# Where a token tile's LayerNorm units, its first projections and the first scores stand in a Trainium2 transformer layer

## The chip, the cores and the metric

The kernel runs on all 8 cores of one Trainium2 chip. Each core computes one of the 8 sequences (2048 tokens of width 1024) with its own copy of the weights; the cores exchange nothing. The metric is device microseconds of the slowest core. Engines have short names: PE is the matrix engine, PEld its weight loads, DVE the vector engine, ACT the scalar engine, POOL and SP two engines that here mostly issue DMAs.

## The reference, cut to what matters

```
x = x + attention(layernorm(x))       # 8 heads of 128, softmax inside blocks of 64 tokens
x = x + spikes(layernorm(x))          # 1024 -> 4096 -> 1024 with squared relu
# attention: q = xn Wq + bq, k = xn Wk + bk, v = xn Wv + bv
#            softmax(q k^T / sqrt(128)) v  per block of 64 tokens, then Wo, bo
# spikes:    h = relu(xn W_fc^T)^2, y = h W_proj^T, five steps of a threshold unit on y
```

Inputs and weights arrive in float32. Weights are turned to bf16 by the DMAs that load them.

## The kernel before

**Tiles and stages.** The 2048 tokens of a core are four tiles (p = 0 to 3) of 512, and a tile is four row units of 128 tokens; unit i belongs to tile i // 4. A unit is loaded as 128 rows of x, normalized and transposed into a quarter of the tile `xnt[p % 2]`. In attention each tile needs 8 q groups, 8 k groups (one per head), 8 v groups and 8 o groups. A group is 8 matmuls of 512 columns into one of three PSUM banks, `ps_m`, which go round. Then come the two matrices of the feed-forward part, whose matmuls are the larger part of the time.

**Order of the work.** Nothing is planned at run time. Each engine has one program in order, and all of them walk the same list: block b = -1 is the q and k groups of tile 0 (`block_keys(-1)`: q0, k0, q1, k1, ... q7, k7 at s = 0 to 15); block 0 is q and k of tile 1 for heads 0 to 3 (s = 0 to 7), v of tile 0 (s = 8 to 15), q and k of tile 1 for heads 4 to 7, and v of tile 1, and then tile 0's o groups. In block b the scores, softmax and values of tile b are woven in between the groups at fixed places: `scores(b, 0)` (heads 0 to 3) stands before s = 0 and `scores(b, 1)` before s = 8 (`scores_four`, L82). The text below writes q0 to k7 for the groups of tile 0 and q(1,0), k(1,0), q(1,1), k(1,1) for the first of tile 1.

**How a unit goes through the engines.** Four steps: `ln_stats` on DVE (L654: two BATCH_NORM_STATS2 and an aggregate), `ln_rstd` on ACT (L554: Ln, then Exp), `ln_scale` on DVE (L662: subtract and multiply into `xn`), and `turn_x` on PE (L344: 8 transposes), whose result `turn_copy` on ACT (L561) copies into `xnt`. Units 4 to 7, those of tile 1, have their places in block -1: `EARLY_TURNS = (8, 11, 13, 15)` says before which s PE transposes them, and `ln_unit` (L133) sets the stats three places earlier, the rstd two, the scale one. Their transposes and that of unit 0 go to the single bank `ps_t`: the next transpose waits until the copy of the one before is done (`turn_free`, L340). Units 1 to 3 have banks of their own.

**Halves.** The first three groups of tile 0 (`HALVED = 3`) are made in halves of 256 tokens (L373): the first halves of q0, k0 and q1, with the transposes of units 2 and 3 between them, and then the second halves. Later tiles' groups take all 512 tokens at once and wait at the tile's first group for all four units (L363).

**ACT's other work.** ACT empties every q and k group with a bias (L566), in the order of the list, and makes the exponentials of the softmax. In its program the copy of a transposed unit stands before the emptying of its place's group, and the rstd of a unit just before the emptying of its group as well.

**Loads.** POOL issues the weights: Wq and Wk head by head, two heads deep (the load of head h waits until that of head h - 2 has landed, L857 to L864), then the two halves of Wv, each behind one of the last two k weights (L866). SP issues the first four units of x, then units 4 to 7 into `xs`, each behind one k weight: unit 4 + i behind head i + 1 (L951). Behind them on SP stand `bo` (waits for the second half of Wv), and the loads `xl` of units 8 onward.

Of the kernel before, what the change touches and what calls it, by code (L numbers as in the profile page):

```python
# [102 lines left out]

HALVED = 3


# [18 lines left out]

EARLY_TURNS = (8, 11, 13, 15)  # L130


def ln_unit(b, s, step):  # L133
# [22 lines left out]
def turn_order():  # L156

    keys = [("x", 0)]
    for b in range(-1, 4):
        for s in range(len(block_keys(b))):  # L160
            if (i := ln_turn(b, s)) is not None:
                keys.append(("x", i))
            if (j := turn_p_pair(b, s)) is not None:
                keys.append(("pt", b, j))
    return {k: n for n, k in enumerate(keys)}


def build_nc():
# [83 lines left out]
    ld_xs = [sem(f"ld_xs{i}") for i in range(4)]  # L252
# [62 lines left out]
    def turned_copied(i):  # L315
        return (free_x, i) if 1 <= i <= 3 else (free_t, turn_no[("x", i)] + 1)
# [22 lines left out]
    def tensor_program(E):  # L339
# [32 lines left out]

        def q_or_k_half(key, half):  # L373

            kind, _, h = key
            w_sb, loaded = (wq_sb, ld_wq) if kind == "q" else (wk_sb, ld_wk)
            if half == 0:
                E.wait_ge(loaded[h], 16)
            if key == ("q", 0, 0):
                E.wait_ge(*turned_copied(2 * half))  # L380
                E.wait_ge(*turned_copied(2 * half + 1))
            for c in range(8):
                k0 = h * 1024 + c * 128
                m = E.matmul(bank(key)[:, half * 256:(half + 1) * 256], w_sb[:, k0:k0 + 128],
                             tokens(xnt[0], c, 2 * half, 2), start=(c == 0), stop=(c == 7))
            return m

        def v_group(key):
# [116 lines left out]
        turn_x(1)  # L505
        for _ in range(WARM_AGAIN):
            E.matmul(ps_m[2][:], attn_sb[:, 0:128], attn_sb[:, 0:512], start=True, stop=True)
        for s, key in enumerate(block_keys(-1)[:HALVED]):
            q_or_k_half(key, 0)
            if s < 2:  # L510
                turn_x(2 + s)
        for b in range(-1, 4):
            for s, key in enumerate(block_keys(b)):
                if (i := ln_turn(b, s)) is not None:
                    turn_x(i)
                if (j := turn_p_pair(b, s)) is not None:
                    turn_p(b, j)
                if (f := scores_four(b, s)) is not None:
                    scores(b, f)
                if (f := values_four(b, s)) is not None:  # L520
                    values(b, f)
                if b == -1 and s < HALVED:
                    q_or_k_half(key, 1).then_inc(filled(key)[0], 1)
                else:
                    main(key)
            if b >= 0:
                for tt in range(4):
                    for half in range(2):
                        main(("o", b, tt, half))
# [23 lines left out]
    def scalar_program(E):  # L553
        def ln_rstd(i):  # L554
            E.wait_ge(ve_var, i + 1)
            E.activation(lnv[i % 2][:], mv[i % 2][:, 1:2], ACT.Ln,  # L556
                         bias=eps_sb[:, 0:1]).then_inc(ac_ln, 1)
            E.wait_ge(ac_ln, i + 1)
            E.activation(rstd[i % 2][:], lnv[i % 2][:], ACT.Exp, scale=-0.5).then_inc(ac_rstd, 1)

        def turn_copy(i):  # L561
            E.wait_ge(*turned(i))
            E.copy(ln_tile(i // 4)[:, i % 4 * 1024:(i % 4 + 1) * 1024],
                   turn_bank(i)).then_inc(turned_copied(i)[0], 1)

        def main(key):  # L566
            E.wait_ge(*filled(key))
            if key[0] == "q":
                h = key[2]
                if key == ("q", 0, 0):  # L570
                    E.wait_ge(ve_bqs, 1)
                    E.wait_ge(ld_bias, 16)
                m = E.activation(q_sb[:, h * 512:(h + 1) * 512], bank(key)[:], ACT.Identity,  # L573
                                 bias=bqs_sb[:, h:h + 1], scale=DKS)
            elif key[0] == "k":
                h = key[2]
                m = E.activation(k_sb[:, h * 512:(h + 1) * 512], bank(key)[:], ACT.Identity,  # L577
                                 bias=bias_sb[:, 8 + h:9 + h])
            else:
                m = E.activation(h_sb[key[2]][:], bank(key)[:], ACT.Relu)  # L580
            m.then_inc(emptied(key)[0], 1)

        def exps(p, j):
            E.wait_ge(free_s, 4 * p + j + 1)
            E.activation(e_sb[:], e_sb[:], ACT.Exp).then_inc(ac_exp, 1)

        def store_x2(p, tt):
            for half in range(2):
                E.wait_ge(*emptied(("o", p, tt, half)))
            j = 4 * p + tt  # L590
            E.dma_start(out=x2_h[j * 128:(j + 1) * 128, :], in_=xr[tt][:]).then_inc(st_x2[tt], 16)

        def value_copy(p, h):
            E.wait_ge(full_v, 4 * p + h // 2 + 1)
            src = bass.AP(values_bank(h)[:].tensor, (h % 2) * 256,
                          [[1024, 128], [512, 2], [64, 4], [1, 64]])
            dst = bass.AP(attn_sb[:].tensor, h * 512, [[4096, 128], [64, 2], [128, 4], [1, 64]])
            E.activation(dst, src, ACT.Identity,
                         bias=bias_sb[:, 16 + h:17 + h]).then_inc(free_v, 1)

        E.dma_start(out=bias_sb[:], in_=bias_h).then_inc(ld_bias, 16)

        E.wait_ge(ve_eps, 1)
        E.activation(table_sb[:], eps_sb[:], ACT.Ln)
        ln_rstd(0)
        ln_rstd(1)
        turn_copy(0)
        turn_copy(1)
        ln_rstd(2)
        ln_rstd(3)  # L610
        turn_copy(2)
        turn_copy(3)
        for b in range(-1, 4):
            for s, key in enumerate(block_keys(b)):
                if (i := ln_turn(b, s)) is not None:
                    turn_copy(i)
                if (f := values_four(b, s)) is not None:
                    value_copy(b, 4 * f)
                    value_copy(b, 4 * f + 1)
                if (i := ln_unit(b, s, LN_RSTD)) is not None:  # L620
                    ln_rstd(i)
                if key[0] != "v":
                    main(key)
                if f is not None:
                    value_copy(b, 4 * f + 2)
                    value_copy(b, 4 * f + 3)
                if (j := softmax_pair(b, s)) is not None:
                    exps(b, j)
            if b >= 0:
                for tt in range(4):  # L630
                    store_x2(b, tt)
        for fc in range(EARLY_UP, 32):
            main(("up", 0, fc))
        for t in range(4):
            if t > 0:
                for fc in range(32):
                    main(("up", t, fc))
            if t < 3:
                i = 20 + 4 * t
                for j in range(4):  # L640
                    ln_rstd(i + j)


    def vector_program(E):
# [119 lines left out]
        for b in range(-1, 4):  # L764
            keys = block_keys(b)
            added = {}
            for s, key in enumerate(keys):
                if (j := softmax_pair(b, s)) is not None:
                    softmax_shift(b, j)
                if (j := turn_p_pair(b, s)) is not None:  # L770
                    p_copy(b, j)
                if (i := ln_unit(b, s, LN_SCALE)) is not None:
                    ln_scale(i)
                if b >= 0 and (i := ln_unit(b, s, LN_BLOCKS)) is not None:
                    ln_blocks(i)
                if (i := ln_unit(b, s, LN_STATS)) is not None:
                    ln_stats(i)
                if s > 0 and (j := softmax_pair(b, s - 1)) is not None:
                    softmax_scale(b, j)
                if key[0] == "v":  # L780
                    v_copy(key)
                if b == 3 and s > 0:
                    square(0, s - 1)
                if b >= 0 and s >= len(keys) - 4:
                    tt = s - (len(keys) - 4)
                    added[tt] = add_bo(b, tt)
# [40 lines left out]
    def gpsimd_program(E):  # L827
# [35 lines left out]
                E.wait_ge(ld_wk[h - 2], 16)  # L863
            w_load(wk_sb[:, hs], wk_h[h], ld_wk[h])  # L864
        for half in range(2):
            E.wait_ge(ld_wk[6 + half], 16)  # L866
            w_load(wv_sb[:, half * 4096:(half + 1) * 4096], wv_h[half], ld_wv[half])

        E.wait_ge(*filled(("v", 0, 0, 0)))
# [36 lines left out]
    def sync_program(E):  # L906
# [41 lines left out]
        for tt in range(4):  # L948
            xr_load(0, tt)
        for i in range(4):  # L950
            E.wait_ge(ld_wk[i + 1], 16)  # L951
            E.dma_start(out=xs[i][:], in_=rows(x_h, 4 + i)).then_inc(ld_xs[i], 16)
        E.wait_ge(ld_wv[1], 16)
        E.dma_start(out=bo_sb[:], in_=bass.AP(bo_h.tensor, 0, [[0, 128], [1, 1024]])).then_inc(ld_bo, 16)
# [113 lines left out]
```

## Time and profile before

| | us |
|---|---|
| time, median of 3 runs (range) | 709.55 (709.0 to 710.76) |
| the profiled execution's own time | 708.54 |
| its span, slowest core (core 2) | 706.9 |
| spans of the 8 cores | 704.4 to 706.9 |
| PE busy in core 2 | 690.8 (98% of the span) |
| DVE, ACT, POOL busy | 384.3, 171.1, 49.9 |
| mean granted clock of PE, all cores | 0.997 to 0.999 of full speed |

The span runs from a core's first to its last instruction. It is shorter by 1.64 us than the time of that execution. An engine's busy share of the whole span says little about a stage, so the rows below are read in order of time: each row of a timeline is a run of equal instructions with its start, the length from the start of the first to the end of the last, and in brackets how long the engine sat idle before it and what released it.

### The profile page before, as it was taken

Reading aid. Unit: us, or ns where it says so; the run is one execution under the profiler, and the core shown is the slowest. Engines: PE = TensorE matmul, PEld = TensorE weight load, DVE = VectorE, ACT = ScalarE, POOL = GpSimd, SP = SyncE. Lnnn points to the kernel's source line nnn. Section 1 sums busy time; section 2 is a strip of 40 time slices with the busy share of each in tenths; the row PEclk is TensorE's granted clock in tenths of the full one; section 3 lists DMA queues with packets and bytes.
Section 4 is the critical chain, followed back from the end, with each engine's and each line's share of the span. In section 5 each row is a group of like instructions: output and inputs, shape, how many; then the busy total and the mean of one; then the engine's idle time right before and its main releaser. Section 6 shows DMA issues by size and latency. Waiting matters only on the chain.

```text
span 706.9 us, 10613 instructions; the slowest of 8 cores (704.4 to 706.9 us)
## 1 busy us (share of the span) xinstructions
PE 690.8 (98%) x3765; PEld 325.0 (46%) x3804; DVE 384.3 (54%) x573; ACT 171.1 (24%) x314; POOL 49.9 (7%) x96
## 2 busy tenths in 40 slices
PE   7999999999999999999999999999999999999996
PEld 3544444444444444444444444444444444444444
DVE  5235765786687466337755226845225865221476
ACT  3553330450351145030003331002332001332000
POOL 2211110121005100000000000000000000000000
PEclk9999999999999999999999999999999999999999
DMA  8997986598659994496361002262002042100011
GB/s 182 195 166 147 168 154 182 120 215 205 157 183 191 254 214 88 136 179 181 108 190 59 1 1 60 62 206 89 1 1 61 36 143 79 40 1 1 31 45 45
DMA packets 31010, 80.92 MB, mean 114 GB/s; under 512 B 5616, under 2 KB 5872, under 8 KB 30192
## 3 DMA queue, kind: packets, MB, share of 16 engines
q0 software_dynamic: 12960, 31.46, 25.4%
q1 hardware_dynamic: 15552, 40.39, 19.3%
q10 hardware_dynamic: 2448, 8.40, 3.0%
q8 instruction: 32, 0.52, 0.3%
q14 instruction: 18, 0.15, 0.1%
HBM read 82.33 MB, written 16.78 MB: 140 GB/s over the span
## 4 chain that ended last, share of the span: by engine, by line
PE 92%; DMA 5%; DVE 1%; issue 1%; DVEq 0%; POOLq 0%
PE ps_m L422 31%; PE ps_y L494 30%; PE ps_m L369 13%; PE ps_m L409 8%; PE ps_m L395 8%; DMA wq_sb<-Wq 5%; DVE acc_sb L738 1%; PE ps_y L448 1%; PE ps_y L476 1%; PE ps_t L460 1%; PE ps_m L501 0%; DVE acc_sb L735 0%; PE ps_t L351 0%; DVE xr L743 0%; DVE attn_sb L753 0%
## 5 line engine op out<-in xcount | busy, mean ns | idle before, releaser
L422 PE MATMUL ps_m<-xn2t,w_sb 128*128 128x512 bf16 x1024 | 223.0, 379 | 0.1
L494 PE MATMUL ps_y<-w_sb,h_sb 128*128 128x512 bf16 (+1 forms) x1001 | 216.4, 376 | 1.2
L422 PEld LDWEIGHTS ps_m<-xn2t,w_sb 128*128 128x128 bf16 x1024 | 99.7, 98 | 119.3 <-issue 0.2
L494 PEld LDWEIGHTS ps_y<-w_sb,h_sb 128*128 128x128 bf16 x1024 | 100.2, 98 | 117.6
L580 ACT ACTIVATE h_sb<-ps_m 128x512 bf16<-128x512 f32 x128 | 76.4, 597 | 267.9 <-PE ps_m L422 267.9
L728 DVE TENSOR_TENSOR h_sb<-h_sb 128x512 bf16<-128x512 bf16 x128 | 53.1, 424 | 125.8 <-ACT h_sb L580 125.7
L738 DVE SCALAR_TENSOR_TENSOR acc_sb<-ps_y,acc_sb 128x1024 bf16<-128x1024 f32 (+2 forms) x72 | 78.6, 1092 | 7.9 <-DVE acc_sb L735 0.5
L369 PE MATMUL ps_m<-xnt,wq_sb 128*128 128x512 bf16 x240 | 56.7, 379 | 2.3 <-DMA wq_sb<-Wq 2.3
L369 PE MATMUL ps_m<-xnt,wk_sb 128*128 128x512 bf16 x248 | 58.6, 379 | 0.0
L395 PE MATMUL ps_m<-wv_sb,xnt 128*128 128x512 bf16 x248 | 55.5, 379 | 0.8 <-issue 0.6
L409 PE MATMUL ps_m<-wo_sb,attn_sb 128*128 128x512 bf16 x249 | 55.4, 379 | 0.4
L735 DVE TENSOR_SCALAR acc_sb<-ps_y 128x1024 bf16<-128x1024 f32 (+2 forms) x18 | 19.5, 1084 | 63.7 <-PE ps_y L494 63.6
L573 ACT ACTIVATE q_sb<-ps_m,bqs_sb 128x512 bf16<-128x512 f32 x32 | 22.0, 686 | 78.1 <-PE ps_m L369 76.3
L409 PEld LDWEIGHTS ps_m<-wo_sb,attn_sb 128*128 128x128 bf16 x256 | 25.0, 98 | 30.2
L723 DVE TENSOR_TENSOR xr<-ps_m,xr 128x512 f32<-128x512 f32 x32 | 22.1, 690 | 29.5 <-PE ps_m L409 29.5
L395 PEld LDWEIGHTS ps_m<-wv_sb,xnt 128*128 128x128 bf16 x256 | 24.6, 98 | 28.5
L369 PEld LDWEIGHTS ps_m<-xnt,wq_sb 128*128 128x128 bf16 x240 | 22.7, 98 | 29.4 <-issue 3.4
L369 PEld LDWEIGHTS ps_m<-xnt,wk_sb 128*128 128x128 bf16 x248 | 23.7, 98 | 26.6 <-issue 0.2
L678 DVE STREAM_TRANSPOSE blk<-xn 128x1024 bf16<-128x1024 bf16 x24 | 29.8, 1241 | 1.5
L709 DVE CAST v_sb<-ps_m 128x512 bf16<-128x512 f32 x32 | 21.8, 685 | 14.1 <-PE ps_m L395 14.1
L556 ACT ACTIVATE lnv<-mv,eps_sb 128x1 f32<-128x1 f32 x32 | 9.4, 293 | 82.3 <-DVE mv L660 82.3
L577 ACT ACTIVATE k_sb<-ps_m,bias_sb 128x512 bf16<-128x512 f32 x32 | 22.0, 687 | 23.5 <-PE ps_m L369 23.2
(63 smaller groups left out, 340.2 us busy)
## 6 DMA issues: line engine op xcount, KB each, us to landing
xr<-x SPq DMA_DIRECT2D x32, 512.0 KB, 6.9
xl<-x SPq DMA_DIRECT2D x96, 128.0 KB, 4.1
w_sb<-Wfc POOLq DMA_DIRECT2D x32, 256.0 KB, 8.9
x<-xr ACTq DMA_DIRECT2D x16, 512.0 KB, 5.2
out<-xr POOLq DMA_DIRECT2D x12, 512.0 KB, 2.9
w_sb<-Wpr POOLq DMA_DIRECT2D x16, 256.0 KB, 32.7
xn2t<-blk SPq DMA_DIRECT2D x64, 64.0 KB, 2.0
w_sb<-Wpr POOLq DMA_DIRECT2D x4, 1024.0 KB, 15.1
```

The costliest lines, as they stand in the source:

```text
L369: m = E.matmul(bank(key)[:], w_sb[:, k0:k0 + 128], tokens(xnt[p % 2], c, 0, 4), start=(c == 0), stop=(c == 7))
L395: m = E.matmul(bank(key)[:], xnt[p % 2][:, tt * 1024 + c * 128:tt * 1024 + (c + 1) * 128], wv_sb[:, k0:k0 + 512], start=(c == 0), stop=(c ...
L409: m = E.matmul(bank(key)[:], attn_sb[:, h * 512 + tt * 128:h * 512 + (tt + 1) * 128], wo_sb[:, k0:k0 + 512], start=(h == 0), stop=(h == 7))
L422: m = E.matmul(bank(key)[:], w1_sb[fc // 4][:, k0:k0 + 128], tokens(xn2t, c, 0, 4), start=(c == 0), stop=(c == 7))
L494: return E.matmul(out, h_sb[fc][:, tt * 128:(tt + 1) * 128], w2_sb[fc // 4][:, k0:k0 + n], start=(fc == 0), stop=(fc == 31))
L573: m = E.activation(q_sb[:, h * 512:(h + 1) * 512], bank(key)[:], ACT.Identity, bias=bqs_sb[:, h:h + 1], scale=DKS)
L577: m = E.activation(k_sb[:, h * 512:(h + 1) * 512], bank(key)[:], ACT.Identity, bias=bias_sb[:, 8 + h:9 + h])
L580: m = E.activation(h_sb[key[2]][:], bank(key)[:], ACT.Relu)
L678: E.transpose(dst[:, :, :, u, :], xn[i % 2][:].rearrange("p (c a t) -> p c a t", c=8, a=4)).then_inc(ve_blk, 1)
L723: E.tensor_tensor(xr[tt][:, hs], bank(key)[:], xr[tt][:, hs], ALU.add).then_inc(emptied(key)[0], 1)
L728: E.tensor_tensor(h_sb[fc][:], h_sb[fc][:], h_sb[fc][:], ALU.mult).then_inc(ve_sq, 1)
L738: m = E.scalar_tensor_tensor(acc, y, level, acc, ALU.is_gt, ALU.add)
```

## The change

Five edits, all of them in the first 60 us of the program.

1. The transposes of units 4 and 5 move from before s = 8 and 11 of block -1 to before s = 11 and 14 (k5 and q7); their stats, rstd and scale move with them.
2. Units 6 and 7 leave block -1. On DVE `ln_stats`, `ln_scale` of unit 6 and then of unit 7 stand at the start of block 0. On ACT `ln_rstd(6)`, `ln_rstd(7)`, `turn_copy(6)`, `turn_copy(7)` stand at the end of block -1, behind the emptying of k7. On PE their transposes stand behind the first halves below.
3. The first three groups of tile 1, q(1,0), k(1,0) and q(1,1), are made in halves of 256 tokens like those of tile 0: the first halves need units 4 and 5 only, and the transposes of units 6 and 7 follow the first and the second of them; then come the second halves.
4. `scores(0, 0)` moves from the start of block 0 to before q6 (s = 12) of block -1. The softmax of these scores stays where it was, in block 0.
5. Units 4 to 7 are asked for behind the k weights of heads 2, 3, 5 and 6 instead of 1, 2, 3 and 4. The halves of Wv wait for units 6 and 7 (`ld_xs[2]`, `ld_xs[3]`) instead of the k weights of heads 6 and 7.

```diff
+FIRST_SCORES = (-1, 12)
-EARLY_TURNS = (8, 11, 13, 15)
+EARLY_TURNS = (11, 14)
@@ turn_order
+        if b == -1:
+            keys += [("x", 6), ("x", 7)]
@@ q_or_k_half
             if half == 0:
-                E.wait_ge(loaded[h], 16)
-            if key == ("q", 0, 0):
-                E.wait_ge(*turned_copied(2 * half))
-                E.wait_ge(*turned_copied(2 * half + 1))
+                if p == 0:
+                    E.wait_ge(loaded[h], 16)
+                main_free(key)
+            if kind == "q" and h == 0:
+                E.wait_ge(*turned_copied(4 * p + 2 * half))
+                E.wait_ge(*turned_copied(4 * p + 2 * half + 1))
@@ tensor_program
-        for s, key in enumerate(block_keys(-1)[:HALVED]):
-            q_or_k_half(key, 0)
-            if s < 2:
-                turn_x(2 + s)
         for b in range(-1, 4):
             for s, key in enumerate(block_keys(b)):
+                if (b, s) == FIRST_SCORES:
+                    scores(0, 0)
+                if b < 1 and s == 0:
+                    for n, halved in enumerate(block_keys(b)[:HALVED]):
+                        q_or_k_half(halved, 0)
+                        if n < 2:
+                            turn_x(4 * (b + 1) + 2 + n)
...
-                if (f := scores_four(b, s)) is not None:
+                if (f := scores_four(b, s)) is not None and (b, s) != (0, 0):
                     scores(b, f)
...
-                if b == -1 and s < HALVED:
+                if b < 1 and s < HALVED:
                     q_or_k_half(key, 1).then_inc(filled(key)[0], 1)
@@ scalar_program, behind the groups of a block
+            if b == -1:
+                ln_rstd(6)
+                ln_rstd(7)
+                turn_copy(6)
+                turn_copy(7)
@@ vector_program, ahead of the groups of a block
+            if b == 0:
+                for i in (6, 7):
+                    ln_stats(i)
+                    ln_scale(i)
@@ gpsimd_program
-            E.wait_ge(ld_wk[6 + half], 16)
+            E.wait_ge(ld_xs[2 + half], 16)
             w_load(wv_sb[:, half * 4096:(half + 1) * 4096], wv_h[half], ld_wv[half])
@@ sync_program
-            E.wait_ge(ld_wk[i + 1], 16)
+            E.wait_ge(ld_wk[(2, 3, 5, 6)[i]], 16)
             E.dma_start(out=xs[i][:], in_=rows(x_h, 4 + i)).then_inc(ld_xs[i], 16)
```

## Rows read from the trace of the kernel before

**Rows 1.** The cores: span and mean granted clock, two of eight.

```profile
core 2: 706.9 us, clock 0.998
core 6: 706.4 us, clock 0.999
```

**Rows 2.** Stretches of core 2: length, busy time by engine, PE clock, DMA share, GB/s.

```profile
10.00:12.00 2.00, 0.49 (x8) 0.46 (x8) 1.82 (x4) 0.50 (x2) 0.00 (x0) 1.00 1.06 176
30.00:40.00 10.00, 8.68 (x52) 4.20 (x51) 3.80 (x7) 5.04 (x10) 2.11 (x4) 1.00 1.06 217
140.00:706.00 566.00, 558.79 (x2914) 259.97 (x2944) 306.92 (x445) 120.45 (x222) 28.13 (x52) 1.00 0.40 102
```

**Rows 3.** Timeline of PE, core 2, units 1 to 3 and the first groups.

```profile
12.28 0.61 PE L351 MATMUL ps_y<-ident,xn 128*128 128x128 bf16 x8 [0.17 <-DVE xn L669]
...
17.69 0.61 PE L351 MATMUL ps_y<-ident,xn 128*128 128x128 bf16 x8
...
19.55 1.03 PE L384 MATMUL ps_m<-xnt,wq_sb 128*128 128x256 bf16 x8 [0.38 <-ACT xnt L563]
...
22.16 1.89 PE L369 MATMUL ps_m<-xnt,wk_sb 128*128 128x512 bf16 x8
23.89 1.89 PE L369 MATMUL ps_m<-xnt,wq_sb 128*128 128x512 bf16 x8
```

**Rows 4.** The same timeline: q5, q6, then unit 7, k7, the scores, q(1,0).

```profile
36.34 1.89 PE L369 MATMUL ps_m<-xnt,wq_sb 128*128 128x512 bf16 x8 [0.76 <-DMA wq_sb<-Wq]
...
41.47 1.89 PE L369 MATMUL ps_m<-xnt,wq_sb 128*128 128x512 bf16 x8 [0.99 <-DMA wq_sb<-Wq]
...
47.09 0.61 PE L351 MATMUL ps_t<-ident,xn 128*128 128x128 bf16 x8
47.53 1.89 PE L369 MATMUL ps_m<-xnt,wk_sb 128*128 128x512 bf16 x8
49.35 0.79 PE L448 MATMUL ps_y<-k_sb,q_sb 128*64 128x64 bf16 x32
50.08 1.90 PE L369 MATMUL ps_m<-xnt,wq_sb 128*128 128x512 bf16 x8
```

**Rows 5.** Timeline of PE, core 6: k1 and q(1,0).

```profile
22.39 1.89 PE L369 MATMUL ps_m<-xnt,wk_sb 128*128 128x512 bf16 x8
...
49.53 1.90 PE L369 MATMUL ps_m<-xnt,wq_sb 128*128 128x512 bf16 x8
```

**Rows 6.** DMA queues of core 2 up to 100 us: packets, MB, share of 16 engines.

```profile
q0 software_dynamic: 4333, 9.47, 61.9%
q1 hardware_dynamic: 2256, 7.34, 26.2%
```

**Rows 7.** Landing times of the tile xs (first row) and of wv_sb (second).

```profile
DMA to landing us min/median/max: 7.4/8.2/9.2
DMA to landing us min/median/max: 10.7/12.1/13.5
```

**Rows 8.** Timeline of POOL, core 2: the issue of the first half of Wv.

```profile
43.22 0.53 POOL L829 DMA_DIRECT2D wv_sb<-Wv  x1 [3.82 <-DMA wk_sb<-Wk]
```

**Rows 9.** Timeline of ACT, core 2: the emptying of q4 and of k7.

```profile
33.95 0.69 ACT L573 ACTIVATE q_sb<-ps_m,bqs_sb 128x512 bf16<-128x512 f32 x1 [1.30 <-PE ps_m L369]
...
49.52 0.69 ACT L577 ACTIVATE k_sb<-ps_m,bias_sb 128x512 bf16<-128x512 f32 x1 [0.58 <-PE ps_m L369]
```

**Rows 10.** Timeline of DVE, core 2: scales and stats of units.

```profile
10.45 1.68 DVE L669 TENSOR_SCALAR xn<-xr,mv,rstd 128x1024 bf16<-128x1024 f32 x2
...
26.60 0.69 DVE L657 BATCH_NORM_STATS2 stat<-xs 128x6 f32<-128x512 f32 x1 [9.40 <-DMA xs<-x]
...
29.06 0.81 DVE L669 TENSOR_SCALAR xn<-xs,mv,rstd 128x1024 bf16<-128x1024 f32 x1 [0.86 <-ACT rstd L559]
...
35.28 0.81 DVE L669 TENSOR_SCALAR xn<-xs,mv,rstd 128x1024 bf16<-128x1024 f32 x1 [1.74 <-ACT rstd L559]
...
75.14 0.68 DVE L657 BATCH_NORM_STATS2 stat<-xl 128x6 f32<-128x512 f32 x1
```

More of the change, by code:

```diff
@@ L373, in q_or_k_half @@
         def q_or_k_half(key, half):
-            kind, _, h = key
+            kind, p, h = key
             w_sb, loaded = (wq_sb, ld_wq) if kind == "q" else (wk_sb, ld_wk)
             if half == 0:
-                E.wait_ge(loaded[h], 16)
-            if key == ("q", 0, 0):
-                E.wait_ge(*turned_copied(2 * half))
-                E.wait_ge(*turned_copied(2 * half + 1))
+                if p == 0:
[4 more added lines that the diff above has]
+                E.wait_ge(*turned_copied(4 * p + 2 * half + 1))
             for c in range(8):
@@ L384, in q_or_k_half @@
                 m = E.matmul(bank(key)[:, half * 256:(half + 1) * 256], w_sb[:, k0:k0 + 128],
-                             tokens(xnt[0], c, 2 * half, 2), start=(c == 0), stop=(c == 7))
+                             tokens(xnt[p % 2], c, 2 * half, 2), start=(c == 0), stop=(c == 7))
             return m
```

## The prediction

> **What bounds the kernel now.** The spans of the cores come first [rows 1], then stretches of core 2 [rows 2]. From 140 us to the end PE is busy 558.8 of 566 us at full clock, so nothing there can be gained or lost except by a shift of the whole. Between 30 and 40 us it is busy only 8.68 of 10 us while the DMA share is full. The PE timeline says why: k1 begins at 22.16 and a group is 1.73 behind the one before it (23.89 - 22.16) [rows 3]. From k1 to k7 there are 12 groups (20.7 us) and four transposes of 0.44 (47.53 - 47.09), so k7 could begin at 44.6. It begins at 47.53: 2.9 us are lost, and q5 and q6 show to what, weights that had not landed [rows 4]. Behind k7 PE runs without a hole to the last matmuls. A test of this: from the start of k(1,1), three groups behind q(1,0), to the end it is 706.9 - 50.08 - 5.18 = 651.6 in core 2 and 706.4 - 49.53 - 5.18 = 651.7 in core 6 [rows 1, 4, 5]. So the forecast needs one number per core, when k(1,1) begins; 651.65 is added to it.
>
> **Part 1, the halves.** The matmuls are the same in number of columns. The last three halves of tile 0 take 22.16 - 19.55 = 2.61, 0.87 each, half of 1.73 [rows 3]. Six halves cost 5.2 like three groups: nothing, on the path or off it. The halves are there to let PE begin tile 1 with two units of four.
>
> **Part 2, the scores and transposes that move.** The 32 small matmuls take 0.73 (50.08 - 49.35) [rows 4] wherever they stand. They need only heads 0 to 3, emptied long before s = 12. DVE looks at them no earlier than now, since its first softmax step stays in block 0, now behind units 6 and 7. Nobody waits for it: PE's next need of it is before s = 8, eight groups on. Zero, with that cover; both ends are 0 to 0.2. Units 4 and 5 are transposed three places later than now, and their rstd lies behind the emptying of q4 and k5, three groups or more before PE wants them: zero.
>
> **Part 3, the loads.** The unit loads leave the stretch in which PE starves. Up to 100 us POOL's queue moved 9.47 MB in 61.9 us of all engines' time and SP's 7.34 MB in 26.2 [rows 6]. A head of Wq or Wk (0.26 MB written) is then 1.7 us and a unit of x (0.52 MB) 1.87 us. Before q5's weights, which land just ahead of 36.34, DMA now carries units 4, 5 and most of 6; after, only 4 and 5. That is 0.85 x 1.87 = 1.6 us earlier, 34.7. PE wants q5 at 22.16 + 7 x 1.73 = 34.3, so 0.5 us of wait remains. Further on two units fewer lie ahead of q6 and one or so ahead of k7, and PE has by then the scores and the transpose of unit 4 before q6: no more wait. The remaining loss r is 0.5, between 0 and the 2.9 of today. So k7 begins at 22.16 + 20.7 + 0.88 (two transposes) + 0.73 (scores) + r = 44.5 + r, where it is 47.5 now. SP's queue has bo and the loads of units 8 and 9 behind this, POOL's the halves of Wv and Wo. The second half of Wv goes out when unit 7 has landed, some 3 us later than now, and takes 10.7 to 13.5 us [rows 7], so it is there by 62; PE wants it after 70. Unit 8 then lands before 71 and DVE wants it at 75.14 [rows 10]. Zero, with 4 us or more of cover; without that each us late would cost one.
>
> **Part 4, what is late next.** Units 6 and 7 now stand behind k7 on every engine, and here new waits arise. I count from the start of k7.
> - ACT may begin `ln_rstd(6)` only behind the emptying of k7, which starts 49.52 - 47.53 = 1.99 behind k7 [rows 4, 9]. From the emptying to the next unit's scale on DVE it is 35.28 - 33.95 = 1.33 [rows 9, 10], the scale takes 0.81, and PE starts a transpose 0.15 after (12.28 against 10.45 + 1.68) [rows 3, 10]. So unit 6 can be transposed at 4.28. PE is at that place at 1.73 + 0.87 = 2.60. **Wait A: 1.7 us.**
> - DVE does unit 6's scale before unit 7's stats. The stats start at 4.13, the scale follows 29.06 - 26.60 = 2.46 later [rows 10], ends at 7.40, and PE may start at 7.55. ACT's copy of unit 6 stands behind `ln_rstd(7)` in its order, and the single bank makes PE wait for that copy too; it ends at about the same time. PE is there at 4.28 + 0.44 + 0.87 = 5.59. **Wait B: 2.0 us.**
> - From the transpose of unit 3 to the second half of q0 it is 19.55 - 17.69 = 1.86 [rows 3]. The second half of q(1,0) thus starts at 9.41, and PE is done with the first half of q(1,1) at 8.86. **Wait C: 0.55 us**, the same as the idle 0.38 printed in the row of q0.
> - k(1,1) begins at 9.41 + 2.61 = 12.02. Behind PE in wait A stand only its own groups; ACT has q(1,0) to empty afterwards and the exponentials, two groups ahead of the bank's next use.
>
> **The sum.** The start of k(1,1) is k1 + 20.7 + 0.88 + 0.73 + r + 12.02 = k1 + 34.35 + r. Core 2: 22.16 + 34.35 + 0.5 = 57.0, against 55.3 now: 3.05 us of weights and of shorter way are won less r, 4.2 us of waits come in. Span 57.0 + 651.65 = 708.7, which is 1.8 above 706.9. Core 6 has k1 at 22.39 [rows 5] and has to wait less for q5: 708.4 to 708.9. The slowest core is about 708.7. The profiled execution would take 708.54 + 1.8 = 710.3. The median shown is 1.0 above that execution, so with the same shift it is 709.55 + 1.8 = **711.3 us**. Against r from 0 to 1.0 and waits that are each some tenths off, the forecast's own range is 710.3 to 712.4.
>
> **Where a page of the skill bears on it.** Units of x landed 7.4 to 9.2 us after they were asked for [rows 7], though each is 1.87 us of work: SP's queue got about a third of the engines' time beside POOL's. The Trainium skill, DMA: Bandwidth & Descriptors, section on queues, rings and completion order, says that each engine takes packets in turn from the rows that have work. By equal turns a unit would land sooner than the row shows, and unit 7 would come some 2 us earlier; the time would be the same, and only the second rival would lose its chance. The row decides.
>
> **Rivals.**
> 1. Units 6 and 7 are ready in time, and only the gain remains. Then k(1,1) stands at k1 + 30.2 + r: 4.2 us less, 707.2. For it speaks that the loads of both are asked for some 9 and 4 us before k7; against it that not the loads but the order on ACT and DVE sets waits A and B, and no row of a step is shorter. Parts of it (a wait half as long) end between 707.2 and 710.
> 2. Slower: unit 7's load is late. It goes out when k6's weights land: now 42.7 (POOL's next issue, 43.22, less its own half us [rows 8]), after the change 1.2 unit loads less lie ahead, so 40.5. With 7.4 to 9.2 us to land [rows 7] it is there at 47.9 to 49.7. DVE is ready for it at k7 + 4.13 = 49.1. Only beyond that does each us late add one to wait B; at 9.2 us plus a late k6 it is 0.6 to 2 us, so 712 to 713.3, in the middle 712.4. What speaks against: unit 7 has at most k7's and q7's weights beside it, fewer than the loads of today had.
> 3. The weights come no earlier, because the engines' time, not the order, is short and the two first unit loads still fall among heads 3 to 5: r is 2.5, 713.3.
> 4. The clock. In the stretch of 10 to 12 us PE is busy 0.49 of 2 us and the granted clock is 1.00 [rows 2]; waits A and B leave no emptier stretch. If the clock fell to its lower level (1.2 of 2.4 GHz), the groups behind k(1,0) would take twice 1.73; for two or three groups that is 3.5 to 5 us, 715 to 716. The Trainium skill, TensorE: Matmul & The Clock Gate, section on why this matters for your kernels, says that a long idle gap between bursts brings the clock down; the row above shows a gap of 1.5 us which didn't.
>
> **Chances.** Forecast 0.64, rival 1 or a part of it 0.13, rival 2 0.15, rival 3 0.05, rival 4 0.03. A measurement of this kernel can tell about 0.3%, 2.1 us, from no change: faster is below 707.4, slower above 711.7. Faster: half of rival 1, 0.06. Slower: some 0.19 of the forecast's own upper part, 0.13 of rival 2, rivals 3 and 4: 0.40. Within: 0.54. The forecast lies within, with its upper end just beyond the bound. The range leaves out rival 4, the end of rival 3 and the lower part of rival 1: 709.3 to 713.1.
>
> **What would show it.** In the profile after: k7 at about 45 in core 2 with one or no wait for weights before it (part 3); PE waiting for DVE's xn at two transposes in `ps_t` behind it, near 1.5 and 1.8 us as printed, and for ACT's xnt once, near 0.4 (part 4); the Ln of unit 6 right behind the emptying of k7; 12 us from k7 to k(1,1); and still 651.65 from there to the end. The stats of unit 7 released by a DMA instead of by DVE's own order would be rival 2; a scale of unit 6 before k7 ends would be rival 1. The forecast is wrong if a core other than 2, 5 or 6 starts k1 much later than 22.4, since every us of k1 is one of the time.

## The result and the profile after

The changed kernel takes 711.98 us in the median of 7 runs (711.34 to 712.84), the kernel before 709.0 beside it; the ratio is 1.0039, 95% interval 1.0025 to 1.0053, about 2.8 us slower (1.8 to 3.8). The forecast was 711.3, 1.8 us slower. In e8 and e10 below, cores 4 to 7 ran at a clock of 0.98 to 0.99, with the kernel before beside them too (715.69 us), so their times are compared only as ratios or over cores 0 to 3. All cores became slower in the profiled execution, from 705.7 to 709.5 on the mean of eight.

The list of the cores, changed kernel:

```profile
core 2: 709.8 us, clock 0.997
...
core 7: 711.1 us, clock 0.995
```

Timeline of PE in core 2, to be held against [rows 3, 4]: k1, q5 with its wait, k7, then the first half of q(1,0), unit 6, the first half of k(1,0), unit 7, the second half of q(1,0), and k(1,1).

```profile
21.47 1.89 PE L374 MATMUL ps_m<-xnt,wk_sb 128*128 128x512 bf16 x8
...
35.02 1.89 PE L374 MATMUL ps_m<-xnt,wq_sb 128*128 128x512 bf16 x8 [0.86 <-DMA wq_sb<-Wq]
...
45.96 1.89 PE L374 MATMUL ps_m<-xnt,wk_sb 128*128 128x512 bf16 x8 [0.29 <-DMA wk_sb<-Wk]
47.68 1.04 PE L391 MATMUL ps_m<-xnt,wq_sb 128*128 128x256 bf16 x8
50.35 0.61 PE L356 MATMUL ps_t<-ident,xn 128*128 128x128 bf16 x8 [1.63 <-DVE xn L685]
50.79 1.04 PE L391 MATMUL ps_m<-xnt,wk_sb 128*128 128x256 bf16 x8
53.52 0.61 PE L356 MATMUL ps_t<-ident,xn 128*128 128x128 bf16 x8 [1.70 <-DVE xn L685]
...
55.38 1.03 PE L391 MATMUL ps_m<-xnt,wq_sb 128*128 128x256 bf16 x8 [0.38 <-ACT xnt L574]
...
58.00 1.89 PE L374 MATMUL ps_m<-xnt,wk_sb 128*128 128x512 bf16 x8
```

Three waits stand where the kernel before had none: 1.63, 1.70 and 0.38 as printed (waits A, B and C of the prediction). The rows of the other seven cores show the same three within 0.01. ACT and DVE in the same core say what PE waits for:

```profile
47.94 0.69 ACT L588 ACTIVATE k_sb<-ps_m,bias_sb 128x512 bf16<-128x512 f32 x1 [1.49 <-PE ps_m L374]
48.53 0.28 ACT L567 ACTIVATE lnv<-mv,eps_sb 128x1 f32<-128x1 f32 x1
...
51.70 0.29 ACT L567 ACTIVATE lnv<-mv,eps_sb 128x1 f32<-128x1 f32 x1 [2.59 <-DVE mv L676]
...
52.19 0.99 ACT L574 COPY xnt<-ps_t 128x1024 bf16<-128x1024 bf16 x1
54.22 1.01 ACT L574 COPY xnt<-ps_t 128x1024 bf16<-128x1024 bf16 x1 [1.04 <-PE ps_t L356]
```

```profile
43.26 0.69 DVE L673 BATCH_NORM_STATS2 stat<-xs 128x6 f32<-128x512 f32 x1 [1.93 <-DMA xs<-x]
...
49.28 0.81 DVE L685 TENSOR_SCALAR xn<-xs,mv,rstd 128x1024 bf16<-128x1024 f32 x1 [4.42 <-ACT rstd L570]
50.01 0.69 DVE L673 BATCH_NORM_STATS2 stat<-xs 128x6 f32<-128x512 f32 x1
...
52.46 0.81 DVE L685 TENSOR_SCALAR xn<-xs,mv,rstd 128x1024 bf16<-128x1024 f32 x1 [0.86 <-ACT rstd L570]
```

Unit 6 had landed, and its stats began, at 43.26. Its scale waited on DVE 4.42 us for an rstd that on ACT stands behind the emptying of k7 (47.94, then the Ln at 48.53). Unit 7's stats began the moment that scale was off DVE, with no DMA in the bracket. Unit 7 was in place 3 us before that, as the issues of SP (the four loads of units, the last one at the end of the row) and POOL (second half of Wv, which waits for unit 7) show:

```profile
22.17 16.75 SPq L972 DMA_DIRECT2D xs<-x  x4
```

```profile
46.99 0.53 POOL L849 DMA_DIRECT2D wv_sb<-Wv  x1 [2.77 <-DMA xs<-x]
```

**Where the time went**, as means over the eight cores of the two profiled executions. k1 starts at 21.2 and at 21.3. From k1 to k7 it was 25.1 us and is 24.4: 0.8 won. From k7 to k(1,1) it was 7.7 and is 12.0: 4.3 lost. From there to the end it was 651.6 and is 651.8: 0.2 lost. Unrounded these add up to the 3.8 between the mean spans. These are one execution of each kernel. Core 7, the slowest, adds something of its own: its wait for q5's weights is longer, and behind it the matmuls themselves are slow.

Timeline of PE, core 7: k4, q5, the transpose of unit 4, k5.

```profile
30.92 1.89 PE L374 MATMUL ps_m<-xnt,wk_sb 128*128 128x512 bf16 x8
35.06 3.19 PE L374 MATMUL ps_m<-xnt,wq_sb 128*128 128x512 bf16 x8 [2.25 <-DMA wq_sb<-Wq]
38.04 1.02 PE L356 MATMUL ps_t<-ident,xn 128*128 128x128 bf16 x8
38.90 1.89 PE L374 MATMUL ps_m<-xnt,wk_sb 128*128 128x512 bf16 x8
```

Stretches of core 7, columns as in [rows 2]; the third number from the end is the granted clock:

```profile
32.00:34.00 2.00, 0.81 (x4) 0.19 (x2) 0.81 (x1) 0.94 (x3) 0.00 (x0) 1.00 1.03 153
34.00:36.00 2.00, 0.94 (x4) 0.46 (x5) 1.35 (x3) 0.00 (x0) 0.53 (x1) 0.87 1.09 173
36.00:38.00 2.00, 2.00 (x6) 0.67 (x5) 0.15 (x1) 0.00 (x0) 0.53 (x1) 0.50 0.98 143
38.00:40.00 2.00, 2.00 (x15) 1.37 (x14) 0.00 (x0) 1.53 (x2) 0.00 (x0) 0.78 1.06 280
```

q5 and the transpose take 3.84 us (38.90 - 35.06) instead of 1.73 + 0.44: 1.7 us lost, at a clock of 0.50 to 0.87, on top of the wait.

### The profile page after: what moved, and what is told of

Its sections match the earlier page's. It is cut to its first block, busy times and chain, and to the rows that moved or that the text cites. A ratio compares the mean times of both kernels' runs of the same rounds, so it can differ in the third digit from the quotient of the medians.

```text
span 711.1 us, 10703 instructions; the slowest of 8 cores (707.9 to 711.1 us)
## 1 busy us (share of the span) xinstructions
PE 695.4 (98%) x3828; PEld 328.1 (46%) x3828; DVE 383.9 (54%) x573; ACT 171.4 (24%) x314; POOL 49.7 (7%) x96
## 4 chain that ended last, share of the span: by engine, by line
PE 93%; DMA 4%; DVE 2%; issue 1%; ACT 0%; POOL 0%; DVEq 0%; ACTq 0%; POOLq 0%
PE ps_m L429 31%; PE ps_y L501 30%; PE ps_m L374 13%; PE ps_m L402 8%; PE ps_m L416 8%; DMA wq_sb<-Wq 4%; DVE acc_sb L754 1%; PE ps_y L455 1%; PE ps_y L483 1%; PE ps_t L467 1%; PE ps_m L508 0%; PE ps_m L391 0%; PE ps_t L356 0%; DVE acc_sb L751 0%; ACT xnt L574 0%
## 5 line engine op out<-in xcount | busy, mean ns | idle before, releaser
L374 PE MATMUL ps_m<-xnt,wk_sb 128*128 128x512 bf16 x240 | 56.7, 379 | 0.0
L374 PE MATMUL ps_m<-xnt,wq_sb 128*128 128x512 bf16 x224 | 54.3, 386 | 2.3 <-DMA wq_sb<-Wq 2.3
```

The source lines that it names most:

```text
L374: m = E.matmul(bank(key)[:], w_sb[:, k0:k0 + 128], tokens(xnt[p % 2], c, 0, 4), start=(c == 0), stop=(c == 7))
```

## The experiments

Two theories at the start. Mine: the waits behind k7 come from the order in which ACT and DVE do units 6 and 7, and the loads matter only before k7. The main rival: unit 7 (or both) is asked for too late. Ratios are to the kernel before, run beside each of them; the changed kernel's own is 1.0039. What is said of single cores is read from one execution of each kernel.

**e1: one step of the order moved.**

```diff
+                if (b, s) == (-1, 14):
+                    ln_rstd(6)
                 if key[0] != "v":
                     main(key)
...
             if b == -1:
-                ln_rstd(6)
                 ln_rstd(7)
```

> The changed kernel with one step moved: on ACT the rstd of unit 6 stands before the emptying of q7 instead of behind that of k7. Theory (the order on ACT and DVE makes waits A and B): unit 6 is ready when PE wants it, wait A (1.63 as printed in the changed kernel) goes to 0; DVE can then start unit 7's stats right after that scale or when the load lands (before 47), so the transpose of unit 7 waits only for the rstd behind k7 and the copy of unit 6, about 0.5 instead of 1.70; the wait for the copy stays 0.38. From k7 to k(1,1) 9 us instead of 12.04, the time 3.1 us less than the changed kernel. Rival (unit 7's load is late): wait A goes but wait B stays at 1.7 or grows, 10.4 us or more from k7 to k(1,1), stats of unit 7 released by a DMA, time 1.7 us less at most.

Ratio 1.0001 (0.9992 to 1.001), 0.4% below the changed kernel. PE in core 2 of this run, from k7 on:

```profile
44.83 1.89 PE L374 MATMUL ps_m<-xnt,wk_sb 128*128 128x512 bf16 x8
...
47.43 0.61 PE L356 MATMUL ps_t<-ident,xn 128*128 128x128 bf16 x8
...
49.41 0.61 PE L356 MATMUL ps_t<-ident,xn 128*128 128x128 bf16 x8 [0.50 <-DVE xn L686]
...
51.27 1.03 PE L391 MATMUL ps_m<-xnt,wq_sb 128*128 128x256 bf16 x8 [0.38 <-ACT xnt L574]
...
53.88 1.89 PE L374 MATMUL ps_m<-xnt,wk_sb 128*128 128x512 bf16 x8
```

Wait A is gone, wait B is 0.50, and k(1,1) comes 9.05 us behind k7: one 0.5 us step on ACT, moved by two places, gives back 3.0 us here and 2.7 on the mean of the eight cores. In six cores the stretch is 8.9 to 9.2 us. In cores 1 and 7 it is 9.9 and 10.4; there late loads appear once the order no longer covers them. In core 7 it is unit 7, as the rival has it; in core 1 it is unit 6, whose stats waited for their load until 44.50 and pass the delay down the chain. DVE, core 7:

```profile
48.47 0.69 DVE L674 BATCH_NORM_STATS2 stat<-xs 128x6 f32<-128x512 f32 x1 [1.08 <-DMA xs<-x]
```

**e2: the loads in the old order.** The two waits of edit 5 are undone, nothing else.

> The changed kernel with the loads in the old order: units 4 to 7 behind the k weights of heads 1 to 4, the halves of Wv behind those of heads 6 and 7. Theory: from k7 to k(1,1) still 12.0 us, since ACT and DVE order and not the loads set it; the waits for weights before k7 come back (3 us in all against about 2 in the changed kernel), so 0.5 to 1.5 us slower than the changed kernel. Rival (late loads cause waits A and B): the stretch from k7 to k(1,1) shrinks to 8 or 9 us and the kernel is 2 to 3 us faster than the changed one.

Ratio 1.0069 (1.0055 to 1.0083), 0.3% or 2.1 us above the changed kernel, somewhat more than expected. PE, core 2: k7, then the transposes of units 6 and 7.

```profile
45.68 1.89 PE L374 MATMUL ps_m<-xnt,wk_sb 128*128 128x512 bf16 x8
...
50.07 0.61 PE L356 MATMUL ps_t<-ident,xn 128*128 128x128 bf16 x8 [1.63 <-DVE xn L685]
...
53.25 0.61 PE L356 MATMUL ps_t<-ident,xn 128*128 128x128 bf16 x8 [1.70 <-DVE xn L685]
```

From k7 to k(1,1) it is 12.04 to 12.05 in every core, with units 6 and 7 asked for at the old, early places. This rules the late loads out as the cause of waits A and B, and shows that edit 5 is worth having inside this change.

**e3: the first scores inside wait A.**

```diff
-                if (b, s) == FIRST_SCORES:
-                    scores(0, 0)
...
                         q_or_k_half(halved, 0)
+                        if (b, n) == (0, 0):
+                            scores(0, 0)
```

> The changed kernel with the first scores not before q6 but behind the first half of q(1,0), inside wait A. Theory: from k7 to k(1,1) stays 12.0 us, wait A shrinks by 0.7 to 0.9 because the scores fill it; k7 begins up to 0.8 us earlier where no weights hold it (they held it in two of eight cores), so 0.3 to 0.8 us faster than the changed kernel. Rival (scores before q6 fill a wait for weights that is there anyway): no difference, within 0.2 us.

Ratio 1.0036 (1.0023 to 1.005). Wait A prints 0.91 in all cores instead of 1.63, and k7 to k(1,1) stays 12.04, so the scores do fill it. The time hardly follows, 0.2 us with an interval of 1 us each way, which leaves both theories standing. In this run q6, q7 or k7 waited for weights in three cores, 0.3 to 0.9 us.

**e4: no halves for tile 1.** Units 6 and 7 are transposed before q(1,0), and its first three groups take 512 tokens each.

> The changed kernel without the halves of tile 1: units 6 and 7 are transposed before q(1,0) and the three groups take all 512 tokens. Theory: the transposes stand where ACT and DVE let them, 4.28 and 7.55 us behind k7, q(1,0) begins at 9.4 and k(1,1) at 14.6 instead of 12.0: 2.6 us slower than the changed kernel. Rival (the halves bring nothing, since the waits are the same): no difference.

Ratio 1.0115 (1.0101 to 1.0129): 5.4 us above the changed kernel, twice what I expected. PE, core 1, from k7:

```profile
46.88 1.89 PE L374 MATMUL ps_m<-xnt,wk_sb 128*128 128x512 bf16 x8
51.27 0.61 PE L356 MATMUL ps_t<-ident,xn 128*128 128x128 bf16 x8 [2.50 <-DVE xn L688]
54.45 1.01 PE L356 MATMUL ps_t<-ident,xn 128*128 128x128 bf16 x8 [2.57 <-DVE xn L688]
56.81 3.57 PE L374 MATMUL ps_m<-xnt,wq_sb 128*128 128x512 bf16 x8 [1.35 <-ACT xnt L577]
60.18 2.00 PE L374 MATMUL ps_m<-xnt,wk_sb 128*128 128x512 bf16 x8
```

```profile
52.00:54.00 2.00, 0.00 (x0) 0.00 (x0) 1.04 (x3) 1.29 (x3) 0.00 (x0) 0.89 0.83 123
...
56.00:58.00 2.00, 1.19 (x3) 0.43 (x4) 0.00 (x0) 0.56 (x1) 0.00 (x0) 0.50 0.84 147
```

The order of the waits is as worked out, but q(1,0) begins 9.9 behind k7 and not 9.4, since the second transpose is already slow (1.01 instead of 0.61). The rest is the clock: with no half group between the waits it falls to half, q(1,0) takes 3.37 instead of 1.73, and k(1,0) is longer as well. k(1,1) stands 16.8 to 17.9 us behind k7 in the eight cores, 2.2 to 3.3 above the 14.6 worked out. The mean clock is 0.991 to 0.993 in the eight cores of the profiled run, and lower than in the changed kernel in every core of the other runs. The halves of the change thus do two things: they put work into the waits, and they keep the clock up.

**e5: the scores alone, in the kernel before.**

```diff
+                if (b, s) == (-1, 12):
+                    scores(0, 0)
...
-                if (f := scores_four(b, s)) is not None:
+                if (f := scores_four(b, s)) is not None and (b, s) != (0, 0):
```

> The kernel before with part 4 alone: the first scores before q6 of block -1 instead of at the start of block 0. Theory: q6 waits 0.6 to 1.3 us for its weights in seven of eight cores of the kernel before, the scores (0.73) fill that wait, so k(1,1) comes 0.6 us earlier and the time is 0.3 to 0.7 us less than before. Rival (it is worth nothing where it stands, since other waits grow by as much): within 0.2 us.

Ratio 0.9987 (0.9979 to 0.9996): 0.9 us faster than the kernel before. It is the one kernel here whose whole interval lies below 1. In core 2 the scores and q6 behind them, against [rows 4]:

```profile
39.94 0.79 PE L448 MATMUL ps_y<-k_sb,q_sb 128*64 128x64 bf16 x32
41.59 1.89 PE L369 MATMUL ps_m<-xnt,wq_sb 128*128 128x512 bf16 x8 [0.86 <-DMA wq_sb<-Wq]
```

In six of eight cores q6 has no wait at all now; in this core it still has, and in core 0 one of 0.91 has come up before q7.

**e6: the loads alone, in the kernel before.** Edit 5 and nothing else.

> The kernel before with part 5 alone: units 4 to 7 asked for behind k weights 2, 3, 5, 6, Wv behind units 6 and 7, everything else in the old order. Theory: unit 7 lands near 46.5 and its rstd stands on ACT before the emptying of k6, its transpose before k7, so PE waits for xn at that transpose until 50 and q(1,0) begins near 53 instead of 50: 2.5 to 3.5 us slower than before. Rival (the weights alone count): the waits for weights shrink and it is 0.5 to 2 us faster.

Ratio 1.009 (1.007 to 1.011), 6.4 us slower: right in sign, and wrong in size and place. PE, core 2: the transposes of units 4 and 6, and k6.

```profile
31.59 0.61 PE L351 MATMUL ps_t<-ident,xn 128*128 128x128 bf16 x8 [1.71 <-DVE xn L669]
...
44.73 0.92 PE L351 MATMUL ps_t<-ident,xn 128*128 128x128 bf16 x8 [3.46 <-DVE xn L669]
45.44 3.29 PE L369 MATMUL ps_m<-xnt,wk_sb 128*128 128x512 bf16 x8
```

I had looked at unit 7 only. Unit 4, asked for one head later and still wanted before s = 8, is late first (1.7 to 4.1 us in the eight cores), then unit 6 in seven of them, and in six of eight cores the mean clock is 0.994 to 0.996. Edit 5 without edits 1 to 3 is harmful.

**e7: e1 with the first scores before q5.** The kernel of e1 with `FIRST_SCORES = (-1, 10)`.

> The kernel of the rstd experiment (unit 6's rstd before the emptying of q7) with the first scores before q5 instead of q6. Theory: in the changed kernel and in that experiment PE waits at q5, 0.8 to 2.7 us in all cores, and nowhere at q6; scores before q5 fill 0.85 of it, so k7 comes 0.8 us earlier where k7's weights do not hold it, the time 0.5 to 0.9 us less than that experiment (ratio near 0.999 to before), and no core falls to the lower clock behind q5. Rival (the stretch is bound by the landing of k7's weights): the wait moves on to q6 or k7, within 0.2 us of that experiment.

Ratio 0.9997 (0.9986 to 1.0008). From k1 to k7 the mean is 22.9 us, against 24.8 in e1 and 24.4 in the changed kernel; q5 waits 0.33 in one core and not at all in the others, and no core shows the lower clock. But unit 7 does not come sooner with k7, so wait B is back to 0.5 to 1.7 (and 0.3 of wait A in core 2), and of 1.9 us won before k7 only part reaches the end. Between this run and e1 the time differs by less than the intervals.

**e8: the scores before q5, in the kernel before.** As e5, with `(-1, 10)`.

> The kernel before with one edit: the first scores stand before q5 of block -1. With them before q6 (the run with the scores alone) PE still waited 0.4 to 1.2 us at q5 in all but one core, and hardly at q6. Theory: before q5 the scores fill that wait, and q6's comes back in part: the same 0.3 to 1.3 us less than before as the scores before q6 gave (0.9 us), give or take 0.3. Rival: the wait at q5 goes and none comes back, 1.5 us or more less than before.

Ratio 0.9995 (0.9983 to 1.0007), by itself no gain that can be told from zero, nor from the 0.13% of e5. Cores 0 to 3 settle it. Over the runs in which their clock was 0.997 or more (13, and 22 of the kernel before), their mean span is 704.97 us against 705.81, which is 0.8 us less, and e5 has the same 0.8 on the mean of its eight cores. q5 waits in two cores (0.24 and 0.35), q6 in five (0.18 to 1.21), so the waits move on to q6 and the gain is that of e5, as the first theory has it.

**e9: unit 5 asked for one head later.** The changed kernel with `(2, 4, 5, 6)` for `(2, 3, 5, 6)`.

> The changed kernel with unit 5 asked for behind k weights 4 instead of 3. Theory (units 4 and 5, both ahead of q5's weights, make its wait): one unit load less, 1.87 us of engines' time, lies ahead of q5; its wait of 0.9 to 2.3 us shrinks to 0 to 0.5, no core's clock falls behind it, and k7 stands nearer to k1: 23.3 instead of 24.4 on the mean; the stretch from k7 to k(1,1) stays 12.04. Time 0.5 to 1.5 us less than the changed kernel. Rival (DMA time as a whole holds k7): q5's wait goes and one at q6 to k7 comes, no difference in time.

Ratio 1.0031 (1.0021 to 1.004), the mean of k1 to k7 23.4 us instead of 24.4, k7 to k(1,1) 12.04. q5 and k7 in core 0:

```profile
33.43 1.89 PE L374 MATMUL ps_m<-xnt,wq_sb 128*128 128x512 bf16 x8
...
44.54 1.67 PE L374 MATMUL ps_m<-xnt,wk_sb 128*128 128x512 bf16 x7 [0.46 <-DMA wk_sb<-Wk]
```

q5 does not wait in any core, so the unit load that was moved had made that wait. A part comes back, as the rival says: q7 or k7 waits for weights in three cores (0.4 to 0.6 us), and in core 1 the transpose of unit 5, now asked for later, waits 0.95. k7 gains 1.0 us in the profiles; in time the intervals of this kernel and the changed one overlap.

**e10: stats of units 6 and 7 first.** e7 with both stats ahead of both scales on DVE.

> The changed kernel with unit 6's rstd before the emptying of q7, the scores before q5, and on DVE the stats of unit 7 before the scale of unit 6. Theory: unit 7's stats no longer stand behind unit 6's scale, so its transpose waits 0 to 0.5 us instead of 0.5 to 1.7; unit 6's scale now stands behind the landing of unit 7 and its transpose waits 0.5 to 1.5 instead of 0 to 0.3. From k7 to k(1,1) 9 us, as before this edit or up to 0.5 less; against the kernel before within 0.2%. Rival (only the second transpose matters): 1 us less.

Ratio 1.0008 (0.9994 to 1.0021). Unit 7's transpose now waits 0.37 or 0.38 in all cores, for the copy of unit 6 and no longer for DVE. Unit 6's waits 0.2 to 0.9 in four cores and hardly in the others, less than the 0.5 to 1.5 expected. k7 to k(1,1) is 8.9 to 10.0. The waits moved and the time did not, as expected: three orders of the same few steps (e1, e7, e10) all end within 0.1% of the kernel before.

## Why the prediction was right, and what it missed

- **The waits behind k7.** Unit 6's transpose was forecast 4.28 us behind k7, unit 7's 7.55, the second half 9.41, k(1,1) 12.02. Measured in core 2: 50.35 - 45.96 = 4.39, 7.56, 9.42, 12.04. e1 and e2 show the cause: the order on ACT and DVE, not the loads.
- **The constant rest.** Forecast 651.65 from k(1,1) to the end; measured 651.8.
- **The halves** cost nothing (the last three take 2.62 us, as forecast) and are needed (e4).
- **The scores** were put at zero, with 0.73 us wherever they stand; before q6 they take 0.85 (39.86 - 39.01 in core 2). e3 gives 0.2 us for the changed kernel, not told from zero. In the kernel before, at the same place, they are worth 0.9 us (e5).
- **The step that failed is the size of r**, the wait for weights that is left before k7. Forecast 0.5 us, measured 24.37 - 22.45 = 1.9 on the mean, 1.6 without core 7 (22.45 is the stretch without a wait, with 0.85 for the scores). The sign named for core 2, one or no wait for weights before k7, failed too: it has three (0.28, 0.86 and 0.29). q5 began 0.6 us earlier than before on the mean (35.4 to 34.8) where I had 1.6. The price of a unit load was right: with one unit load fewer ahead of q5 (e9), POOL's next issue behind q5's weights comes 1.8 us sooner, against 1.87 forecast. What was off, by that price, was the count: how much of the third unit's load had been carried before q5's weights landed. The 0.85 of the prediction, for which it shows no row, roughly fits core 2, where POOL's issue behind those weights comes 1.4 us sooner (36.62 to 35.22); on the mean it is 0.7, about a third of a unit. This count is argued from the dates, no experiment varied it. In core 2 the weights came about when forecast (q5 at 35.0), but k1 began 0.7 earlier, and PE only waited longer for them. So the last sentence of the prediction was too strong: a us of k1 is a us of the time only where the weights come later by as much. Mostly they do: the four cores of the changed kernel that start k1 later, by 1.0 us on the mean, start q5 0.7 later.
- **That 1.4 us is more than the miss in the total** (2.8 against 1.8). The intervals of the two times, 1 us each way, don't let the rest be split. That the forecast came so near was in part luck. In core 2, 1.7 us too little for r and 0.15 for the rest were offset by a k1 that began 0.7 earlier (span 709.8, forecast 708.7). The profiled execution took 712.81, 2.5 above the 710.3 forecast for it, but it was one of the slower of its kernel. And the 711.3 started from a median of 709.55 for the kernel before, which is 709.0 with more runs, so the time is missed by 0.7 and the change by 1.0.
- **Rival 4, the clock, was given too small a chance.** I argued from a single stretch that waits of this size don't bring it down. Waits A and B didn't; the wait of 2.25 before q5 did, in the slowest core of the profiled execution. By the mean clock (0.995 there, 0.997 or more elsewhere) it is one core of 56 over the seven runs of the changed kernel, so it moves the profiled time and hardly the median.
- **Rival 2** did not decide. k6's weights landed at about 38.6 (the last issue of SP's row ends at 38.9) and not 40.5, and unit 7 was there before 46.99, some 8 us after being asked for, as [rows 7] has it. By equal turns of the queues, the rule of the Trainium skill's page DMA: Bandwidth & Descriptors (queues, rings and completion order), it would have been sooner still by the prediction's estimate; the row decided rightly. DVE wanted unit 7 only at 50.01, so its load had 3 us to spare.
- **Rival 3** had the better size for r: 1.9 lies nearer to its 2.5 than to my 0.5, and e9 shows its mechanism, a unit load ahead of q5's weights, at work. Only the waits before q6 went as I had it; before k7 two cores wait 0.3. I gave it 0.05, too little.
- **Rival 1** is out: both waits came in all cores.

## What to carry to other kernels

When work is put off to be closer to its use, follow every step of it on every in-order engine: here the loads were early enough, and a 0.5 us step queued behind one eviction cost 2.7 us. Start dates that depend on a DMA and on an engine should be forecast as the later of the two, core by core, and not as a sum. A small independent piece of work can be worth more than a large rearrangement when it fills a hole that exists already: the scores alone, before q6, beat both kernels (ratio 0.9987), while in wait A they filled the hole and the time did not show it (e3). The rest of the change, even with its order mended, only comes back to where the kernel before was.

## What the runs showed of the hardware

The clock of PE can fall to its lower level inside a kernel that is otherwise dense. A single wait of 2.25 (changed kernel, core 7) and one of 2.71 us (e3, core 7) were followed by stretches at a granted clock of 0.50 to 0.61. One of 2.40 (e1, core 6), one of 3.35 (e6, core 1) and the pairs of 1.63 and 1.70 with 1.3 us of work between were not (1.00 throughout). So between 2.25 and 3.35 us the length of the wait alone did not decide it here. Waits of 2.50 and 2.57 with only a transpose between brought it down in every core of e4, in cores 5 and 6 already behind the first. It costs 1.7 us (changed kernel, core 7) to 3.3 us (e4, core 7) beyond the waits. The Trainium skill, TensorE: Matmul & The Clock Gate, section on what is actually happening, has the two levels and that the clock depends on how busy PE has lately been; the rows agree (1.00 and 0.50).
